# Dense blocks of 34 tiles from five node regions, in a two-layer graph network on one core

## The chip, the core and the metric

One core of a Trainium2 chip runs the whole program. The metric is the device time of one execution in microseconds (us); lower is better. TensorE multiplies matrices, VectorE and ScalarE work element by element, GpSimd (POOL) issues the gathers, SyncE (SP) issues most other DMAs.

## The reference

There are 12,500 nodes with 128 features and 200,000 edges with 64 attributes; `dst` is sorted, and dst = 12500 u^2 with u uniform, so nodes of low number have many edges and the rest few. Biases and weights of two layers follow.

```python
h = relu(layernorm(x))
for W_msg, Wih, Whh, bih, bhh in layers:                 # two
    msg = concat([h[src], edge_attr], -1) @ W_msg.T
    agg = segment_sum(msg, dst, 12500)
    h = gru_cell(agg, h, Wih, Whh, bih, bhh)
out = x + h
```

The kernel sums `h[src]` and `edge_attr` per node first and multiplies by `W_msg` afterwards, which is the same by linearity. `src` is random over all nodes.

## The kernel before, in words

**Edges.** A tile is 128 consecutive edges, a group four tiles (512 edges); there are 390 full groups and a last one of 320 edges. For a group VectorE makes one-hot matrices of each edge's node within a window of 80 columns (`onehot_of`, L1033 and L1036), TensorE multiplies attributes (L720, layer 0 only: the sum of attributes per node, `edgeT`, serves both layers) and gathered rows (L736) with them into PSUM, and VectorE adds the window into `edgeT` (L1098) and `aggT` (L1101).

**Gathers.** The rows `h[src]` of a group come by four indirect DMAs of 128 rows each, which GpSimd issues (L601) into a ring of six groups (`rows`). It waits for the group six gathers back to be summed and for the group's indices.

**Dense tiles.** The first 78 groups (312 tiles, nodes 0 to 494) are not gathered. All nodes' h lies in SBUF (`hr`, 100 tiles of 125 nodes), and one iteration of the main loop (13 per layer) treats a block of 24 dense tiles. For each tile a matrix A counts how many edges lead from each of the 12,500 nodes to each of 5 columns (nodes) of the tile: `lo_hot` (position within 125 nodes) times `v_hot` (which of the 100 node tiles, times column), made on VectorE (L1015, L1022) and multiplied on TensorE in packs of six tiles (`build_pack`, L689, bf16). ScalarE copies a pack from PSUM to `a_blk` (L1273). Then 100 multiplications of `a_blk` (120 columns) with `hr` (L696) accumulate the block's 120 rows in `ps_v`. This is done in eight slices of 12 or 13 node tiles. At the end ScalarE copies the rows (L1286), TensorE moves them into a window of 128 columns (L766) and VectorE adds it to `aggT` (L1125).

**Order of one iteration.** It is written out by `order(layer)`: 24 gathered groups (`gi` 0 to 23), in layer 0 with 6 attribute-only groups of dense edges between them. After gathered group gi, `divmod(gi, 3)` gives slice and phase: in phases 0 and 1 TensorE builds two packs each, in phase 2 it multiplies the slice. After every sixth gathered group (a step) the chunks whose nodes are complete are computed.

**Chunks.** A chunk is 250 nodes (50 in all): TensorE turns h (L811), multiplies messages (L815, L816) and six gate matrices (L819 to L828), ScalarE copies and applies sigmoid and tanh (L1333 to L1346), VectorE combines (L1178 to L1189), and TensorE turns the result back (`turn_back`, L800) when the next chunk starts. The result goes to a table in DRAM, from which layer 1 gathers, or to the output. `ready_i`, a table made on the chip, says after which step each chunk is ready. Chunks run in the order of nodes, rotated by `ROT`, so that those with dense nodes come last; `last_chunks` treats what is left behind the last group.

**Queues.** SP loads attributes, `dst_in` and indices into slots that come free when `group_summed` passes (`slot_free`), in the order of the groups. VectorE makes the one-hots of a group two places ahead of its addition (`onehot_after`).

**Start.** Layer norm of all nodes, storing them to `h_table` (the gathers wait for that), then tables of the groups' bases and of the dense tiles, made on VectorE from `dst` and `src` (L896 to L974). A tile wider than its columns, or a group wider than its window, would be done again in overflow passes, and all chunks would wait for them.

## Time and profile before

| | us |
|---|---|
| median of 3 runs | 3468.92 |
| lowest, highest | 3451.53, 3472.8 |
| profiled execution | 3465.33 |
| its span, first to last instruction | 3463.4 |
| busy: TensorE, VectorE, ScalarE, GpSimd | 2764.6, 1477.5, 1010.2, 2472.9 |

The profile is of one execution. Its rows name a line of the kernel, an engine, an operation and tiles; PE is TensorE's matmul, PEld its weight load, DVE VectorE, ACT ScalarE, POOL GpSimd. "Idle before" is the idle time of an engine ahead of such an instruction, with what released it; "issue" is time in which it waited for nothing that the profile shows. PEclk is the granted TensorE clock as a share of 2.4 GHz. An f32 matmul stands as two records, a bf16 one as one.

### The profile page before, as it was taken

Reading aid. Unit: us, or ns where it says so; the run is one execution under the profiler, and the core shown is the slowest. Engines: PE = TensorE matmul, PEld = TensorE weight load, DVE = VectorE, ACT = ScalarE, POOL = GpSimd, SP = SyncE. Lnnn points to the kernel's source line nnn. Section 1 sums busy time; section 2 is a strip of 40 time slices with the busy share of each in tenths; the row PEclk is TensorE's granted clock in tenths of the full one; section 3 lists DMA queues with packets and bytes.
Section 4 is the critical chain, followed back from the end, with each engine's and each line's share of the span. In section 5 each row is a group of like instructions: output and inputs, shape, how many; then the busy total and the mean of one; then the engine's idle time right before and its main releaser. Section 6 shows DMA issues by size and latency. Waiting matters only on the chain.

```text
span 3463.4 us, 74591 instructions
## 1 busy us (share of the span) xinstructions
PE 2764.6 (80%) x20436; PEld 2489.4 (72%) x20437; DVE 1477.5 (43%) x4429; ACT 1010.2 (29%) x2007; POOL 2472.9 (71%) x2544
## 2 busy tenths in 40 slices
PE   0788888988898998989867777778776878777886
PEld 0787877877887787778746767777776767766775
DVE  6543444444444444444423333333343444444443
ACT  5322222322233333332322122222222323233333
POOL 4677777777777777767527777777777777777772
PEclk9988888988988988988867677777787888888887
DMA  7333333333333333323233222222222222222221
GB/s 190 78 86 85 90 86 86 93 87 85 92 87 88 92 90 80 93 78 86 74 72 80 53 58 56 59 58 59 59 61 59 61 62 61 61 64 65 63 59 35
DMA packets 367262, 262.22 MB, mean 76 GB/s; under 512 B 239960, under 2 KB 325596, under 8 KB 366962
## 3 DMA queue, kind: packets, MB, share of 16 engines
q0 software_dynamic: 81376, 167.62, 17.8%
q1 hardware_dynamic: 264807, 70.52, 10.0%
q10 hardware_dynamic: 20779, 20.48, 2.0%
q8 instruction: 139, 2.28, 0.3%
q14 instruction: 161, 1.32, 0.1%
HBM read 239.14 MB, written 19.20 MB: 75 GB/s over the span
## 4 chain that ended last, share of the span: by engine, by line
PE 37%; POOL 31%; issue 16%; DVE 5%; ACT 3%; DMA 3%; DVEq 2%; ACTq 2%; POOLq 1%; SPq 0%
POOL rows L601 31%; PE ps_v L696 11%; PE ps_win L736 9%; PE ps_win L720 4%; PE ps_c L689 2%; PE ps_a L819 2%; PE ps_q L689 2%; DVEq L1093 1%; PE ps_c L823 1%; PE ps_c L821 1%; PE ps_b L824 1%; PE ps_d L826 1%; DMA rows<-h_table,idx 1%; ACT hr L1255 1%; PE ps_d L828 1%
## 5 line engine op out<-in xcount | busy, mean ns | idle before, releaser
L601 POOL DMA_INDIRECT rows<-h_table,idx x1252 | 1229.1, 982 | 481.9 <-issue 404.8
L601 POOL DMA_INDIRECT rows<-x_table,idx x1252 | 1219.0, 974 | 445.1 <-issue 433.9
L736 PE MATMUL ps_win<-onehot,rows 128*128 128x80 f32 x5008 | 801.8, 311 | 235.6 <-DMA rows<-x_table,idx 169.9
L736 PEld LDWEIGHTS ps_win<-onehot,rows 128*128 128x128 f32 x5008 | 716.8, 220 | 282.7 <-issue 169.2
L696 PE MATMUL ps_v<-hr,a_blk 125*120 125x128 f32 x5200 | 817.9, 330 | 0.0
L696 PEld LDWEIGHTS ps_v<-hr,a_blk 125*120 125x120 f32 x5200 | 796.8, 238 | 0.0
L1273 ACT COPY a_blk<-ps_q 125x390 f32<-125x390 f32 (+1 forms) x416 | 220.6, 530 | 1176.1 <-PE ps_q L689 1079.5
L1022 DVE SCALAR_TENSOR_TENSOR v_hot<-v_cur,lane 128x390 bf16<-128x390 f32 (+1 forms) x834 | 422.6, 544 | 0.0
L1101 DVE TENSOR_TENSOR aggT<-aggT,ps_win 128x80 f32 x626 | 143.8, 230 | 579.1 <-PE ps_win L736 520.8
L720 PE MATMUL ps_win<-onehot,attr 128*64 128x80 f32 x3128 | 317.7, 252 | 67.1 <-issue 44.0
L1036 DVE TENSOR_TENSOR onehot<-lane,rel 128x320 f32<-128x320 f32 x706 | 348.8, 494 | 24.2
L689 PE MATMUL ps_q<-v_hot,lo_hot 128*125 128x65 bf16 (+1 forms) x2496 | 226.6, 230 | 145.8 <-DVE v_hot L1022 141.0
L720 PEld LDWEIGHTS ps_win<-onehot,attr 128*64 128x64 f32 x3128 | 259.5, 148 | 102.8 <-issue 59.1
L1098 DVE TENSOR_TENSOR edgeT<-edgeT,ps_win 64x80 f32 x391 | 89.5, 229 | 560.0 <-PE ps_win L736 493.6
L689 PEld LDWEIGHTS ps_q<-v_hot,lo_hot 128*125 128x125 bf16 x2496 | 202.0, 151 | 161.8 <-DVE v_hot L1022 155.9
L1178 DVE SCALAR_TENSOR_TENSOR r_sb<-ps_a,bT,r_sb 128x250 f32<-128x250 f32 x100 | 47.8, 478 | 519.1 <-ACT r_sb L1337 300.7
L689 PE MATMUL ps_c<-v_hot,lo_hot 128*125 128x65 bf16 (+1 forms) x2496 | 236.8, 235 | 6.7 <-DVE v_hot L1022 6.7
L1273 ACT COPY a_blk<-ps_c 125x390 f32<-125x390 f32 (+1 forms) x416 | 220.5, 530 | 14.2 <-PE ps_c L689 10.5
L1273 ACT ACT_TABLE_LOAD x104 | 133.4, 1283 | 278.5 <-PE ps_q L689 277.4
L689 PEld LDWEIGHTS ps_c<-v_hot,lo_hot 128*125 128x125 bf16 x2496 | 199.5, 153 | 12.2 <-DVE v_hot L1022 8.5
L1033 DVE TENSOR_SCALAR rel<-dst_in,base_all 128x4 f32<-128x4 int32 x706 | 171.5, 243 | 12.1 <-issue 8.9
L1323 ACT ACT_TABLE_LOAD x100 | 128.3, 1283 | 89.3 <-issue 89.0
(178 smaller groups left out, 1940.8 us busy)
## 6 DMA issues: line engine op xcount, KB each, us to landing
attr<-in_edge_attr_dram SPq DMA_DIRECT2D x390, 128.0 KB
rows<-h_table,idx POOLq DMA_INDIRECT x1252
rows<-x_table,idx POOLq DMA_INDIRECT x1252
dst_in<-in_dst_dram SPq DMA_DIRECT2D x702, 2.0 KB
idx<-in_src_dram SPq DMA_DIRECT2D x624, 2.0 KB
x_table<-out_sb ACTq DMA_DIRECT2D x50, 125.0 KB
attr<-in_x_dram ACTq DMA_DIRECT2D x50, 125.0 KB
out_dram<-out_sb ACTq DMA_DIRECT2D x50, 125.0 KB
```

Source lines behind the costliest of these rows:

```text
L601: nc.gpsimd.indirect_dma_start(out=rows[0:parts, s, j, :], out_offset=None, in_=table[:, :], in_offset=bass.IndirectOffsetOnAxis(ap=idx[0: ...
L689: mm = nc.tensor.matmul((ps_q, ps_c)[k % 2][0:QUART, j * wide:(j + 1) * wide], lo_hot[:, k * PACK + j, :], v_hot[:, k % 2, j, 0:wide], sta ...
L696: mm = nc.tensor.matmul(ps_v[0:VC, 0:H], a_blk[:, t - slice_at[sl], :], hr[:, t, :], start=(t == 0), stop=(t == NT - 1))
L720: mm = nc.tensor.matmul(ps_win[r % 2][0:D, WIN:2 * WIN], attr[0:parts, r, j, :], onehot[0:parts, r % 2, j, :], start=(j == 0), stop=(j == ...
L736: mm = nc.tensor.matmul(ps_win[r % 2][:, 0:WIN], rows[0:parts, rr, j, :], onehot[0:parts, r % 2, j, :], start=(j == 0), stop=(j == TILES - 1))
L1022: return nc.vector.scalar_tensor_tensor(out=v_hot[:, k % 2, :, 0:wide], in0=cur[:, k * PACK:(k + 1) * PACK].unsqueeze(2).to_broadcast([P, ...
L1033: nc.vector.tensor_scalar(rel[:, s % 2, :], dst_in[:, s, :], float(N), base_all[:, bass.ds(g, 1)], ALU.min, ALU.subtract).then_inc(rel_rea ...
L1036: nc.vector.tensor_tensor(onehot[:, s % 2, :, :], lane[:, 0:WIN].unsqueeze(1).to_broadcast([P, TILES, WIN]), rel[:, s % 2, :].unsqueeze(2) ...
L1098: ins = nc.vector.tensor_tensor(e, e, ps_win[s % 2][0:D, WIN:2 * WIN], ALU.add)
L1101: ins = nc.vector.tensor_tensor(a, a, ps_win[s % 2][:, 0:WIN], ALU.add)
L1273: return nc.scalar.copy(a_blk[:, 0:n, k * PACK * W:(k + 1) * PACK * W].rearrange("p h (j w) -> p j h w", w=W), (ps_q, ps_c)[k % 2][0:QUART ...
L1323: nc.scalar.activation(scratch[:, :], zero[:, :], ACT.Sigmoid)
```

## The change

Dense tiles become 408 (102 groups, nodes 0 to 849), taken from five regions of nodes: a block has 8 tiles of 2 columns, 7 of 3, 8 of 4, 7 of 5 and 4 of 6, that is 34 tiles and 128 columns; its tiles of a region are consecutive, those of different regions far apart. There are 12 iterations for 13, and seven slices (14 or 15 node tiles) for eight, in the first 21 of 24 gathered places. A pack is a list of parts of regions (`PACK_TILES`), so each of VectorE's and ScalarE's operations on a pack becomes one per part: seven per slice for four. The block's window (now five pieces of `aggT`) moves from the end of the iteration to the 22nd gathered place. Of the 102 dense groups' attributes, 8 stand in each iteration and 6 (`HEAD`) ahead of the loop. The rings of attributes and `dst_in` shrink from six to four slots. ROT goes from 2 to 4. The tables at the start are made per region. In a chunk, the message matmuls come before the previous chunk's `turn_back`, `h_rows` is copied one chunk ahead, the result is written to `z_sb` rather than over `m_sb`, and a chunk starts when the previous one's `t_ready` has come. SP issues the last group's index load before its wait.

```diff
-ITERS = 13
+ITERS = 12
 SUBS = 4
 SLOTS = SUBS * RING
-ROT = 2
-W = 5
-BT = RING * TILES
-VC = BT * W
-PACK = 6
-PACKS = BT // PACK
-SLICES = 8
+ROT = 4
+AR = 4
+REGIONS = ((8, 2, 14), (7, 3, 20), (8, 4, 32), (7, 5, 36), (4, 6, 26))
+PACK_TILES = (((0, 0, 8), (1, 0, 6)), ((3, 6, 7), (4, 0, 4)), ((2, 0, 8),), ((1, 6, 7), (3, 0, 6)))
+NR = len(REGIONS)
+TILE_AT = [sum(n for n, w, c in REGIONS[:r]) for r in range(NR + 1)]
+ROW_AT = [sum(n * w for n, w, c in REGIONS[:r]) for r in range(NR + 1)]
+COL_AT = [sum(c for n, w, c in REGIONS[:r]) for r in range(NR + 1)]
+BT = TILE_AT[NR]
+VC = ROW_AT[NR]
+PACKS = len(PACK_TILES)
+SLICES = 7
+USED = 3 * SLICES
...
-    DENSE = ITERS * RING
+    DENSE = ITERS * BT // TILES
+    ATTR = SLOTS // (AR - 1)
+    HEAD = DENSE - ITERS * ATTR
...
-        dst_in = sb("dst_in", [P, RING, TILES], I32)
+        dst_in = sb("dst_in", [P, AR, TILES], I32)
         rel = sb("rel", [P, 2, TILES])
         rows = sb("rows", [P, RING, TILES, H])
-        attr = sb("attr", [P, RING, TILES, D])
+        attr = sb("attr", [P, AR, TILES, D])
...
-        v_hot = sb("v_hot", [P, 2, PACK, HS * W], BF16)
+        v_hot = sb("v_hot", [P, 2, HS * max(sum((b - a) * REGIONS[r][1] for r, a, b in rs) for rs in PACK_TILES)], BF16)
...
-            return [(q, None, q // 5) if q % 5 == 4 else (q, q - q // 5, None) for q in range(SLOTS + RING)]
+            return [(q, None, q // AR) if q % AR == AR - 1 else (q, q - q // AR, None) for q in range(SLOTS + ATTR)]
 
         def place(layer, it, q):
 
-            return it * len(order(layer)) + q
+            return it * len(order(layer)) + q + (0 if layer else HEAD)
...
+        def pack_parts(sl, k):
+
+            at = 0
+            for r, a, b in PACK_TILES[k]:
+                n, w = b - a, REGIONS[r][1]
+                wide = (slice_at[sl + 1] - slice_at[sl]) * w
+                yield TILE_AT[r] + a, ROW_AT[r] + a * w, n, w, wide, slice(at, at + n * wide)
+                at += n * wide
...
-                sp.wait_ge(group_summed, p + (layer * ORDERED[0] - RING + 1 + AHEAD))
+                sp.wait_ge(group_summed, p + (layer * ORDERED[0] - AR + 1 + AHEAD))
...
+                for t, row, n, w, wide, at in pack_parts(sl, k):
+                    for j in range(n):
+                        own = slice(at.start + j * wide, at.start + (j + 1) * wide)
+                        mm = nc.tensor.matmul((ps_q, ps_c)[k % 2][0:QUART, own], lo_hot[:, t + j, :],
+                                              v_hot[:, k % 2, own], start=True, stop=True)
                 return mm
...
-                    pe.wait_ge(h_ready, cc)
+                    pe.wait_ge(h_ready, cc + 1)
                     pe.wait_ge(chunk_done, cc)
                     for q in range(NQ):
-                        tr = nc.tensor.transpose(ps_t[:, q * P:(q + 1) * P], halves(m_sb[:, :])[:, q, :], ident[:, :])
+                        tr = nc.tensor.transpose(ps_t[:, q * P:(q + 1) * P], halves(z_sb[:, :])[:, q, :], ident[:, :])
                     tr.then_inc(h_turned, 1)
 
                 def chunk(i, groups_done, blocks_done, packs_done):
                     cc = layer * CHUNKS + i
                     c = chunk_at(i)
-                    with pe.If(i > 0):
-
-                        turn_back(cc)
-                    pe.wait_ge(h_rows_kept, cc + 1)
+                    pe.wait_ge(t_ready, cc + 1)
+                    pe.wait_ge(h_rows_kept, cc + (layer + 1))
...
+                    with pe.If(i > 0):
+
+                        turn_back(cc)
...
+                    for p in range(HEAD):
+                        attr_group(p, p % AR, p // AR)
...
+                            if gi >= USED:
+                                if gi == USED:
+                                    window_of_block(blk)
+                            elif phase < 2:
...
+            for r, (n, w, c) in enumerate(REGIONS):
+                for to, ps in ((lo_t, ps_a), (drel_t, ps_c)):
+                    nc.vector.tensor_copy(in_blocks(to[:, 0:NTILE])[:, :, tiles_of(r)], region_tiles(ps, r))
+                nc.vector.tensor_copy(in_blocks(hi_t[:, 0:NTILE])[:, :, tiles_of(r)], region_tiles(ps_b, r))
+                nc.vector.tensor_copy(in_blocks(tile_base)[:, :, tiles_of(r)], region_tiles(ps_d[0:1, :], r))
+                nc.vector.tensor_reduce(v_wide[:, :, r], region_tiles(ps_v[0:VC, :], r), AX.X, ALU.max)
+                nc.vector.tensor_reduce(v_min[:, :, r], region_tiles(ps_d[0:VC, :], r), AX.X, ALU.min)
+                nc.vector.tensor_reduce(v_max[:, :, r], region_tiles(ps_d[0:VC, :], r), AX.X, ALU.max)
+                nc.vector.tensor_reduce(region_of[:, r:r + 1], row_of[:, tiles_of(r)], AX.X, ALU.add)
+                ins = nc.vector.tensor_tensor(v_work[:, :, tiles_of(r)], region_tiles(ps_d[0:VC, :], r),
+                                              row_col[:, tiles_of(r)].unsqueeze(1).to_broadcast([VC, ITERS, n]), ALU.add)
...
+                for t, row, n, w, wide, at in pack_parts(sl, k):
+                    ins = nc.vector.scalar_tensor_tensor(
+                        out=v_hot[:, k % 2, at].rearrange("p (t c) -> p t c", c=wide),
+                        in0=cur[:, t:t + n].unsqueeze(2).to_broadcast([P, n, wide]),
+                        scalar=float(slice_at[sl] * w),
+                        in1=lane[:, 0:wide].unsqueeze(1).to_broadcast([P, n, wide]),
+                        op0=ALU.subtract, op1=ALU.is_equal)
...
+                    starts = [dve.value_load(window_base[0:1, bass.ds(it * NR + r, 1)], min_val=0, max_val=N) for r in range(NR)]
+                    added_before(p)
                     dve.wait_ge(v_summed, blk + 1)
-                    a = aggT[:, bass.ds(at, XWIN)]
-                    nc.vector.tensor_tensor(a, a, ps_v[:, 256:256 + XWIN], ALU.add).then_inc(acc_free, 1)
+                    for r, (n, w, c) in enumerate(REGIONS):
+                        a = aggT[:, bass.ds(starts[r], c)]
+                        if r:
+                            dve.drain()
...
-                    nc.vector.tensor_tensor(m_sb[:, :], m_sb[:, :], r_sb[:, :], ALU.add).then_inc(h_ready, 1)
-
-                for q in range(2):
...
+                    act.wait_ge(h_ready, cc + 1)
+                    act.wait_ge(hch_turned, cc + 1)
+                    nc.scalar.copy(h_ch[:, :], ps_h).then_inc(hch_kept, 1)
+                    act.wait_ge(msg_ready, cc + 1)
+                    nc.scalar.copy(m_sb[:, :], ps_m).then_inc(m_kept, 1)
...
+                    keep_rows(i + 1)
+                    if layer == 0:
+
+                        nc.scalar.copy(cols(aggT, c), zero[:, 0:1].to_broadcast([P, CHUNK])).then_inc(agg_cleared, 1)
```

## Rows read from the trace of the kernel before

**Rows 1.** The page, busy us, share of the span and instructions by engine.
```profile
PE 2764.6 (80%) x20436; PEld 2489.4 (72%) x20437; DVE 1477.5 (43%) x4429; ACT 1010.2 (29%) x2007; POOL 2472.9 (71%) x2544
```

**Rows 2.** Windows: length; PE, PEld, DVE, ACT, POOL busy (x); PEclk, DMA share, GB/s.
```profile
200.00:1200.00 1000.00, 875.88 (x7106) 794.00 (x7105) 447.78 (x1381) 272.78 (x538) 763.35 (x777) 0.86 0.34 88
1200.00:1743.00 543.00, 492.51 (x3797) 428.91 (x3795) 246.41 (x752) 177.83 (x362) 374.38 (x384) 0.87 0.32 82
1800.00:3200.00 1400.00, 1057.67 (x7318) 978.34 (x7318) 555.85 (x1509) 372.84 (x707) 1065.65 (x1095) 0.78 0.26 63
...
1655.00:1675.00 20.00, 19.24 (x201) 18.20 (x202) 12.15 (x39) 8.03 (x15) 13.46 (x14) 1.00 0.38 92
```

**Rows 3.** The page, costliest groups: busy, mean ns of one, idle before by releaser.
```profile
L601 POOL DMA_INDIRECT rows<-h_table,idx x1252 | 1229.1, 982 | 481.9 <-issue 404.8
...
L1022 DVE SCALAR_TENSOR_TENSOR v_hot<-v_cur,lane 128x390 bf16<-128x390 f32 (+1 forms) x834 | 422.6, 544 | 0.0
...
L1036 DVE TENSOR_TENSOR onehot<-lane,rel 128x320 f32<-128x320 f32 x706 | 348.8, 494 | 24.2
```

**Rows 4.** Timeline of TensorE: one step of layer 0 (start, length, line).
```profile
1654.89 0.77 PE L720 MATMUL ps_win<-onehot,attr 128*64 128x80 f32 x8
...
1667.64 0.48 PE L689 MATMUL ps_q<-v_hot,lo_hot 128*125 128x60 bf16 x6
...
1668.40 0.77 PE L720 MATMUL ps_win<-onehot,attr 128*64 128x80 f32 x8
...
1675.14 0.47 PE L800 MATMUL ps_d<-ident,m_sb 128*125 128x128 f32 x2
```

**Rows 5.** Timeline of TensorE: the matmul that ends a block, two layers.
```profile
214.38 0.49 PE L766 MATMUL ps_v<-v_onehot,v_rows 120*128 120x128 f32 x2
...
1455.56 0.49 PE L766 MATMUL ps_v<-v_onehot,v_rows 120*128 120x128 f32 x2
...
1742.91 0.49 PE L766 MATMUL ps_v<-v_onehot,v_rows 120*128 120x128 f32 x2
...
3154.17 0.49 PE L766 MATMUL ps_v<-v_onehot,v_rows 120*128 120x128 f32 x2 [0.36 <-ACT v_rows L1286]
...
3410.15 0.49 PE L766 MATMUL ps_v<-v_onehot,v_rows 120*128 120x128 f32 x2 [0.36 <-ACT v_rows L1286]
```

**Rows 6.** Who GpSimd waited for in layer 0: us, times, longest.
```profile
POOL rows L601 <- PE ps_win L736: 60.3, 71, 9.3
```

**Rows 7.** Timeline of VectorE in the table stage, and of GpSimd at the first wait.
```profile
83.18 0.17 DVE L946 COPY lo_t<-ps_a 128x24 f32<-128x24 f32 x1
...
84.81 0.48 DVE L949 TENSOR_REDUCE aggT<-ps_v 120x13 f32<-120x312 f32 x1
...
110.88 1.14 POOL L601 DMA_INDIRECT rows<-h_table,idx  x1 [8.50 <-PE ps_win L736]
```

**Rows 8.** Timeline of TensorE: two chunks in one step of layer 0.
```profile
1640.58 0.47 PE L800 MATMUL ps_d<-ident,m_sb 128*125 128x128 f32 x2
...
1648.30 0.50 PE L800 MATMUL ps_d<-ident,m_sb 128*125 128x128 f32 x2 [2.71 <-DVE m_sb L1189]
```

**Rows 9.** Weight loads by line: count, ns min/median/max, first and last start, shapes.
```profile
L696 PEld LDWEIGHTS ps_v<-hr,a_blk x5200: 183/183/324, 119.4 to 3409.4; 125*120 125x120 f32 x193
...
L736 PEld LDWEIGHTS ps_win<-onehot,rows x5008: 186/192/338, 108.1 to 3422.6; 128*128 128x128 f32 x192, 80*128 80x128 f32 x1
```

**Rows 10.** Chunks at a layer's end: two starts in layer 0, one loop in layer 1.
```profile
1770.01 0.79 PE L800 MATMUL ps_d<-ident,m_sb 128*125 128x128 f32 x2 [2.68 <-DVE m_sb L1189]
...
1780.40 0.79 PE L800 MATMUL ps_d<-ident,m_sb 128*125 128x128 f32 x2 [2.68 <-DVE m_sb L1189]
...
3441.75 0.37 ACT L1333 COPY h_ch<-ps_a 128x250 f32<-128x250 f32 x1 [2.28 <-issue]
...
3448.76 0.42 DVE L1189 TENSOR_TENSOR m_sb<-m_sb,r_sb 128x250 f32<-128x250 f32 x1
```

**Rows 11.** The chain that ended last, around the first gather of layer 1.
```profile
1791.96 2.58 DMA x_table<-out_sb
```

312 lines of the change are left out of this document (181 added, 131 removed).

## Prediction

> **What bounds the kernel now.** I read the busy shares first, and they name the wrong engine: TensorE 80% of the span, GpSimd 71% [rows 1]. Stretches by stage correct this. From 200 to 1200 us GpSimd issued 777 gathers, one every 1.287 us; from 1800 to 3200 us 1095, one every 1.279 us [rows 2]. The costliest groups show why: an indirect DMA keeps GpSimd 0.98 us, and 404.8 us of issue (0.3 us for most) stand before 1252 of them, with no releaser named [rows 3]. So GpSimd never rests there, although its share is only 0.76: the 0.3 us is not counted as busy. TensorE has slack: where its granted clock is 1.00 [rows 2], one step (six gathered groups, two slices of the block) takes it 20.3 us, from 1654.89 to 1675.14 [rows 4], so an iteration of four steps 81 us without chunks, while its 96 gathers take 123 us.
>
> Late in layer 0 this turns. The matmul of L766, which ends each block, stands at 214.38, 1455.56 and 1742.91 us [rows 5]: the last two iterations take 143.7 us each, and the twelve together 1528.5 us where 12 x 96 x 1.279 is 1473. The excess is 55 us. GpSimd's own waits agree: 60.3 us for TensorE in this layer [rows 6], of which 8.5 stand at the start [rows 7]. Nodes per edge grow with the edge number, so the chunks (the GRU of 250 nodes) crowd at the end. Two in one step cost TensorE 14.3 us (1640.58 to 1654.89 [rows 8, 4]), 2.7 of them waiting for the first one's result. In layer 1 the marks 3154.17 and 3410.15 enclose two iterations of 128.0 us [rows 5], together 10 us over their gathers.
>
> **1. Gathers removed: -246 us.** Dense tiles go from 312 to 408, so gathered groups from 24 x 13 to 24 x 12 in each layer: 24 groups of 4 DMAs fewer. 96 x 1.287 + 96 x 1.279 = 246.3 us [rows 2], all on the path as long as GpSimd sets the pace. A gather's rows are as long as before, so its price stays.
>
> Does everything fit? I counted on the inputs that the reference draws: no tile is wider than its region's 2, 3, 4, 5 or 6 nodes, in no block does a region reach over its 14, 20, 32, 36 or 26 columns (the most are 9, 14, 23, 27 and 18), and no group spans 80 nodes. So no overflow pass runs, before or after. The chunks per step, counted in the same way, keep their pattern (2, 1, 2, 1 in the last iteration); five instead of three are left for the end, as ROT goes from 2 to 4.
>
> **2. Start: +17 us (8 to 26).** The gathers begin at the same time: they wait for the stored h_table. But 24 DMAs fill the ring, and GpSimd then waits 8.50 us for the first group to be summed [rows 7]. That group comes later now, and nothing hides it, since the ring is full. First the tables: about 45 VectorE operations by region replace ten over 312 columns; one over 24 columns takes 0.17 and one over 312 takes 0.48 us [rows 7], so 84 or 96 columns about 0.22, and 45 x 0.22 - 10 x 0.48 is +5; some 15 more small ones add 3. I take +8 (bounds 3 and 12, if they overlap more or less than those rows). Then six groups of edge attributes stand ahead of the first gathered one. On TensorE one takes 0.77 us at full clock [rows 4] and under twice that at half; on VectorE the one-hot of the group two places on takes 0.49 [rows 3] and its two neighbours about as much together. Six at 1.5 us are 9 (bounds 5 and 14).
>
> **3. TensorE's work per iteration: +5 us, hidden except late.** Packs: 34 x 7 = 238 small matmuls for 192, in 28 packs for 32. A pair of packs takes 0.76 us (1667.64 to 1668.40, 12 matmuls) [rows 4]; split as 0.053 a matmul and 0.12 a pair that is 14.3 for 12.2, +2.1 (1 if all is per pack, 3 if all is per matmul). Two more attribute groups of 0.7: +1.4. The hundred multiplications load 128 weight columns for 120: the medians of such loads are 192 and 183 ns [rows 9], 200 records, +1.5 to +1.8. VectorE: 49 v_hot operations for 32, on 12,800 columns for 12,000: 32 x 0.544 = 17.4 [rows 3] grows to between 18.6 and 21.5 us (17 more starts of 0 to 0.17), and lo_hot of ten more tiles brings it to about +5 in an iteration of 123 us of which VectorE works 45%. That and ScalarE's copies in two parts lie beside gathers; late in layer 0, where they would not, I count nothing for them and leave the upper end of the range to them.
>
> **4. Chunks reordered: -3 and -4 us.** The message matmuls come ahead of turn_back, h_rows is copied one chunk ahead, and the result goes to z_sb, so a second chunk's front no longer waits for the first one's end. What is left as a loop runs from the copy of h_ch to the last VectorE operation, 3441.75 to 3449.18, 7.4 us; starts now are 10.4 us apart (1770.01, 1780.40) [rows 10]. So each double step of layer 0 (five of them, two in the last iteration) gains 3 us, and the window, moved to the 22nd gathered place, takes about 2 us of waiting off each iteration's end. Against them stand the +5 us of part 3, 6 with its stretches at half clock: the last iteration comes out at 143.7 + 6 - 2 - 6 = 142 us, and the 55 us of excess at about 52: -3. The same in layer 1, without attributes, makes 6 of 10: -4.
>
> **5. Ends of the layers: -2 us.** Five chunks of 7.4 for three of 10.4: +6 a layer. The last three gathered groups carry no pack or multiplication any more, and the last step's chunk need not wait for the block's sum: -4 in layer 0, where TensorE lags by a whole ring, -10 in layer 1, where it lags by one multiplication. The tail's index load ahead of SP's wait frees GpSimd earlier, which is worth nothing: TensorE is later.
>
> **6. Slower gathers: +6 us.** VectorE is busy 448 of 1000 us in layer 0 and 556 of 1400 (397 in 1000) in layer 1, and a gather takes 8 ns longer in layer 0 [rows 2]. Part 3 adds some 4.5 points of VectorE to both: at most 7 ns on 2312 gathers, 16 us; 0 if the 8 ns come from the attribute transfers, and below that if the ring of four spreads these better, which nothing here prices. I take 6.
>
> **Sum:** -246 + 17 - 3 - 4 - 2 + 6 = -232. The profiled execution took 3465.3 us (span 3463.4 and 1.9 around it); the median of the runs is 3468.9, 0.1% above it. 3465.3 - 232 = 3233 us.
>
> **Rivals.**
> - **TensorE takes over (14%).** The chunk reordering gains nothing while part 3 costs its 6 us per iteration. Then the last two iterations take 150 instead of 142 (+16), the three before them 135 instead of 126 (+27), and layer 1 keeps its 10 us (+4): 3233 + 47 = 3280. For it: TensorE is 0.91 busy from 1200 us on [rows 2]. Against it: 2.7 us of each double step are plain waiting [rows 8].
> - **Its stalls vanish (8%).** Late in layer 0 the granted clock is 0.87 [rows 2]. If TensorE pauses so little that it stays at 2.4 GHz, four steps of 21.5 us and six chunks of 5 to 7 fit into the gathers' 123 us, and 45 of the 52 us go: 3188.
> - **Ports (6%).** Each added microsecond of VectorE stops GpSimd for as long: 5 x 24 = 120 us, 0.78 of it beside gathers, 94 less the 6 already counted: 3321. Against it: 51 us more of VectorE in 1000 would then lengthen a gather by 65 ns, and the difference of the layers is 8 [rows 2].
> - **Slower: the ring of four (4%).** SP may load dst_in only two places ahead of VectorE's need, not four. Places pass in 3.84 us in layer 0 (123 / 32) and 5.1 in layer 1. From a free slot to the landed data 2 x 3.84 less 1 us for VectorE are hidden, 6.7 us; beyond, half of the excess is paid on each of 391 places. From 7.9 us the 232 us are used up: 3465, and 3500 at 8.1. Against it: the nearest row is a store of 125 KB that landed 2.6 us after its issue [rows 11].
> - **It does not fit (1%).** One tile over its width would send every chunk behind the last gather: 2 x 45 x 7.4 = +666. The count on the inputs excludes it.
>
> On "ports" the Trainium skill has a rule that speaks against this change. SBUF — State Buffer, "Who interferes with whom", says that a VectorE instruction with two SBUF inputs, or in a two-port mode, and a GpSimd instruction that needs the shared ports exclude each other for a whole instruction; the added one-hots have two SBUF inputs. By that rule the sum would be the rival's, 3321; this case's 8 ns bear out little of it, by which it is 3233.
>
> [...]
>
> **Chances and range.** My forecast has 67% and a range of its own, 3205 to 3260 (start 8 to 26, chunk period 6 to 9, excess 40 to 65 us). The whole range goes from "stalls vanish" with the cheaper start, 3180, to "TensorE takes over" with the dearer start and 16 us of slower gathers, 3310 rounded; ports, ring and misfit, 11%, stay outside. Faster by over 1%: 0.95; within 1%: 0.02; slower by over 1%: 0.03. About 1% is what a measurement of this kernel tells from no change.
>
> **What would show it.** Right: 1156 gathers per layer, one each 1.28 to 1.295 us; GpSimd's wait at the start 24 to 27 us; block marks 123 us apart until the eighth iteration and 138 to 145 in the last two of layer 0; five chunks at each layer's end 7 to 8 us apart; layer 1's first gather at about 1691 us (1795.6 - 123.6 + 17 - 3 + 2 + 3). Wrong: waits of VectorE for dst_in, a mean gather over 1.0 us, marks more than 130 us apart in layer 1.

## The result, and the profile after

The changed kernel takes 3280.1 us in the median of four runs (3269.6 to 3287.8), the kernel before 3465.7 us (four runs): a ratio of 0.9467, 95% interval 0.9426 to 0.9508. That is 186 us less. The forecast was 3233 us, 232 less than before's profiled execution; the time lies in its range (3180 to 3310) and above the likeliest case's own range (3205 to 3260). In the profiled execution the time is 3279.4 us, its span 3277.7.

The page of the kernel after: busy time by engine (against [rows 1]), then its costliest groups (against [rows 3]: busy, mean ns of one, idle before).

```profile
PE 2630.1 (80%) x20375; PEld 2360.7 (72%) x20376; DVE 1530.0 (47%) x4895; ACT 999.1 (30%) x2343; POOL 2324.6 (71%) x2389
...
L666 POOL DMA_INDIRECT rows<-h_table,idx x1156 | 1153.2, 998 | 485.3 <-issue 376.2
L666 POOL DMA_INDIRECT rows<-x_table,idx x1156 | 1144.5, 990 | 410.4 <-issue 402.1
...
L1115 DVE SCALAR_TENSOR_TENSOR v_hot<-v_cur,lane 128x42 bf16<-128x42 f32 (+13 forms) x1180 | 435.1, 425 | 0.0
...
L1130 DVE TENSOR_TENSOR onehot<-lane,rel 128x320 f32<-128x320 f32 x682 | 338.2, 496 | 23.4
```

The gathers are 1156 for 1252 in each layer, but each keeps GpSimd 998 and 990 ns instead of 982 and 974. Windows of the kernel after, the columns as in [rows 2]:

```profile
200.00:1200.00 1000.00, 886.69 (x7442) 799.41 (x7442) 492.82 (x1597) 284.81 (x674) 761.56 (x765) 0.86 0.35 89
1200.00:1660.00 460.00, 412.64 (x3412) 361.74 (x3412) 230.13 (x735) 157.82 (x372) 315.89 (x319) 0.90 0.33 84
1800.00:3200.00 1400.00, 1103.20 (x7962) 1008.21 (x7961) 616.46 (x1823) 412.67 (x952) 1070.14 (x1083) 0.79 0.24 60
```

A gather starts every 1.307 us in layer 0's first stretch and every 1.293 in layer 1, for 1.287 and 1.279 before. VectorE is busy 4.5 points more, as forecast. The rest shows in GpSimd's start, its waits (us in total, times, longest) and the matmul that ends each block, now L832, whose start is called a block's mark below (against [rows 7], [rows 6] and [rows 5]):

```profile
82.71 0.94 POOL L666 DMA_INDIRECT rows<-h_table,idx  x1 [0.30 <-issue]
117.79 1.12 POOL L666 DMA_INDIRECT rows<-h_table,idx  x1 [34.14 <-PE ps_win L786]
```
```profile
POOL rows L666 <- PE ps_win L802: 49.7, 77, 7.7
POOL rows L666 <- PE ps_win L786: 36.0, 7, 34.1
POOL rows L666 <- DMA idx<-in_src_dram: 31.7, 6, 13.4
```
```profile
226.41 0.43 PE L832 MATMUL ps_v<-v_onehot,v_rows 128*128 128x128 f32 x2
...
1377.31 0.43 PE L832 MATMUL ps_v<-v_onehot,v_rows 128*128 128x128 f32 x2
...
1520.86 0.43 PE L832 MATMUL ps_v<-v_onehot,v_rows 128*128 128x128 f32 x2
...
1660.00 0.43 PE L832 MATMUL ps_v<-v_onehot,v_rows 128*128 128x128 f32 x2
...
3217.04 0.43 PE L832 MATMUL ps_v<-v_onehot,v_rows 128*128 128x128 f32 x2
```

GpSimd stops after 8 gathers (82.71 is the eighth), not after 24, for 34.14 us. The last two iterations of layer 0 take 143.6 and 139.1 us (forecast: 142), but the nine before them 127.9 each (1377.31 less 226.41, by nine), where 123 was forecast up to the eighth. The first and last gathers of each layer give the account:

```profile
L666 POOL DMA_INDIRECT rows<-h_table,idx x1156: 892/944/1869, 73.0 to 1665.8; - x193
L666 POOL DMA_INDIRECT rows<-x_table,idx x1156: 896/944/1877, 1723.1 to 3220.8; - x193
```

Before, these times were 72.5 to 1736.3 and 1795.6 to 3400.4, and the span ended at 3463.4.

| stretch, us | before | after | change | forecast |
|---|---|---|---|---|
| start to first gather | 72.5 | 73.0 | +0.5 | 0 |
| layer 0, first to last gather | 1663.8 | 1592.8 | -71.0 | -106.6 |
| to layer 1's first gather | 59.3 | 57.3 | -2.0 | with the end: -2 |
| layer 1, first to last gather | 1604.8 | 1497.7 | -107.1 | -123.7 |
| to the end | 63.0 | 56.9 | -6.1 | |

So layer 0 fell short by 36 us and layer 1 by 17, and the ends gave 6 more than forecast.

### The profile page after: what moved, and what is told of

Read it like the earlier page. It is cut to its first block, busy times and chain, and to the rows that moved or that the text cites. A ratio compares the mean times of both kernels' runs of the same rounds, so it can differ in the third digit from the quotient of the medians.

```text
span 3277.7 us, 74395 instructions
## 1 busy us (share of the span) xinstructions
PE 2630.1 (80%) x20375; PEld 2360.7 (72%) x20376; DVE 1530.0 (47%) x4895; ACT 999.1 (30%) x2343; POOL 2324.6 (71%) x2389
## 3 DMA queue, kind: packets, MB, share of 16 engines
q1 hardware_dynamic: 254617, 70.47, 10.3%
## 4 chain that ended last, share of the span: by engine, by line
PE 35%; POOL 30%; issue 16%; DVE 6%; DVEq 4%; DMA 3%; ACT 3%; ACTq 1%; SPq 1%; POOLq 1%
POOL rows L666 30%; PE ps_v L762 9%; PE ps_win L802 8%; PE ps_win L786 4%; PE ps_q L755 3%; DVEq L1187 2%; PE ps_c L755 2%; PE ps_b L879 1%; PE ps_b L880 1%; PE ps_d L866 1%; PE ps_d L895 1%; ACT hr L1366 1%; PE ps_a L886 1%; DVEq L1217 1%; PE ps_c L888 1%
## 5 line engine op out<-in xcount | busy, mean ns | idle before, releaser
L666 POOL DMA_INDIRECT rows<-h_table,idx x1156 | 1153.2, 998 | 485.3 <-issue 376.2
L666 POOL DMA_INDIRECT rows<-x_table,idx x1156 | 1144.5, 990 | 410.4 <-issue 402.1
L762 PE MATMUL ps_v<-hr,a_blk 125*128 125x128 f32 x4800 | 715.2, 319 | 0.0
L762 PEld LDWEIGHTS ps_v<-hr,a_blk 125*128 125x128 f32 x4800 | 698.4, 235 | 0.8
L1385 ACT COPY a_blk<-ps_q 125x224 f32<-125x224 f32 (+5 forms) x504 | 223.8, 480 | 856.3 <-PE ps_q L755 763.7
L1115 DVE SCALAR_TENSOR_TENSOR v_hot<-v_cur,lane 128x42 bf16<-128x42 f32 (+13 forms) x1180 | 435.1, 425 | 0.0
L755 PE MATMUL ps_q<-v_hot,lo_hot 128*125 128x28 bf16 (+5 forms) x3696 | 289.4, 222 | 139.9 <-DVE v_hot L1115 117.7
L755 PEld LDWEIGHTS ps_q<-v_hot,lo_hot 128*125 128x125 bf16 x3696 | 272.5, 151 | 151.2 <-DVE v_hot L1115 128.9
L1385 ACT COPY a_blk<-ps_c 125x70 f32<-125x70 f32 (+7 forms) x672 | 208.3, 376 | 15.1 <-PE ps_c L755 11.1
L755 PE MATMUL ps_c<-v_hot,lo_hot 128*125 128x70 bf16 (+3 forms) x2016 | 200.3, 244 | 6.5 <-DVE v_hot L1115 6.5
```

Source lines behind the costliest of these rows:

```text
L666: nc.gpsimd.indirect_dma_start(out=rows[0:parts, s, j, :], out_offset=None, in_=table[:, :], in_offset=bass.IndirectOffsetOnAxis(ap=idx[0: ...
L755: mm = nc.tensor.matmul((ps_q, ps_c)[k % 2][0:QUART, own], lo_hot[:, t + j, :], v_hot[:, k % 2, own], start=True, stop=True)
L762: mm = nc.tensor.matmul(ps_v[0:VC, 0:H], a_blk[:, t - slice_at[sl], :], hr[:, t, :], start=(t == 0), stop=(t == NT - 1))
L1115: ins = nc.vector.scalar_tensor_tensor(out=v_hot[:, k % 2, at].rearrange("p (t c) -> p t c", c=wide), in0=cur[:, t:t + n].unsqueeze(2).to_ ...
L1385: ins = nc.scalar.copy(a_blk[:, 0:hs, row:row + n * w].rearrange("p h (j w) -> p j h w", w=w), (ps_q, ps_c)[k % 2][0:QUART, at].rearrange( ...
```

## The experiments

Eleven edited kernels ran, and the changed kernel once more (e12_after_again), in three sets of four: e1 to e4, e5 to e8, e9 to e12. Each set has the kernel before timed on the same chip (3472.6, 3464.1 and 3467.7 us), so sets are compared by the ratio to it.

### A wait of the first iteration, and the indices

The place of a group in the order of sums counts the six head groups now. For gathered groups 2 to 5 of the first iteration this makes the wait for a free slot of rows a wait for sums of head groups, though the slots are empty. The first edit drops it; the second loads next iteration's indices earlier.

```diff
+                        if layer == 0 and gi < RING:
+                            with pool.If(it > 0):
+                                pool.wait_ge(group_summed, place(layer, it, rows_free(gi)) + (1 + AHEAD))
+                        else:
+                            pool.wait_ge(group_summed, place(layer, it, rows_free(gi)) + (layer * ORDERED[0] + 1 + AHEAD))
```


> The kernel after, with one edit: in layer 0's first iteration the first six gathered groups no longer wait for sums of the head attribute groups (their slots of rows are empty then). Theory (the unplanned part of the loss at the start is this wait): GpSimd issues 24 gathers instead of 8 before it first waits, that wait falls from 34.1 us to 20 to 25, the first block mark moves from 226.4 to about 218 us and the whole is 8 to 9 us shorter (about 3271 against 3279). Rival (TensorE, with the head groups ahead of its first gathered group, sets the pace there): the first block mark stays within 2 us of 226.4, later waits for TensorE take what the first gives, and the time stays within 3 us.

```diff
-                        if gi == SLOTS - 1:
+                        if gi == SLOTS - (1 if layer else 4):
```


> The kernel after, with one edit: in layer 0 the edge indices of the next iteration's first six groups are loaded after the loads for gathered group 20 and not after those for group 23, so that they wait for the sum of place 22 and not of place 26. Theory: the waits of GpSimd for indices inside the loop (18.3 us in five) are a loss of their own, since with a ring of four the index load of the next iteration is issued two sums later than its slot of rows comes free; they vanish and layer 0's gathers end 8 to 12 us earlier. Rival: TensorE is what is late there; the same time shows up as waits for ps_win, and the time stays within 3 us.

e1_start: 3276.4 us, ratio 0.943 (0.9409 to 0.9451); e2_idx: 3283.3 us, 0.9453 (0.9419 to 0.9488). Both intervals overlap the changed kernel's. In e1_start GpSimd issues its 24 gathers and then waits once:

```profile
102.29 0.94 POOL L666 DMA_INDIRECT rows<-h_table,idx  x1 [0.30 <-issue]
125.36 1.90 POOL L666 DMA_INDIRECT rows<-h_table,idx  x1 [22.12 <-PE ps_win L806]
```

The first block mark stands at 216.8 us for 226.4. Yet the ninth mark is at 1244.0 in e1_start and 1243.9 after, and layer 0's last gather ends at 1667.9 for 1666.7: the lead is given back in the eighth and ninth iteration. GpSimd's first wait is 12 us shorter, its later waits in layer 0 are 8 us longer together. The theory was right on the wait; of the time it named, this trace keeps nothing, though the ratio (0.943 for 0.9467) leaves up to 13 us open. In e2_idx the waits for indices vanish (31.7 us in total become 0.3). The tail's 13.1 us come back as a wait with no releaser named, those for TensorE grow from 49.7 to 58.4, and what is left, 8 us in layer 0, is met by gathers that are 7 us longer in sum in that profile; so little is within what two profiles of one kernel differ. The rival fits: in layer 0 something other than GpSimd is late.

### Is it TensorE's work?

This kernel leaves half of the edge attributes out of layer 0's sums, so it doesn't compute the reference; it is run for its time.

```diff
                 def attr_sums(r, parts):
-                    for j in range(TILES):
+                    for j in range(2):
```


> The kernel after, but TensorE sums the attributes of only two of the four tiles of each group in layer 0 (half of the edge attributes are left out of the sums); transfers, one-hots and additions stay. TensorE works some 10 us less in each of layer 0's iterations, nothing else changes. Theory (from about 900 us on TensorE sets layer 0's pace, which is why what GpSimd gained at the start was given back): the waits of GpSimd for ps_win in the loop nearly vanish, block marks are 126 us apart or less to the end, and layer 0's gathers, 1593.7 us in all after, take 1550 to 1560. Rival (GpSimd sets it, and the waits are noise of the ring): they take over 1580. Layer 1 stays as it is by both.

e5_light: 3289.3 us, ratio 0.9497 (0.948 to 0.9514), layer 0's gathers 1599.1 us to the end of the last (1593.7 in the changed kernel). Nothing is gained, as the rival has it, but its reason, waits that are noise, is not shown: GpSimd's waits in layer 0 after the first add up to 65.7 us for 54.4. Windows of e5_light:

```profile
200.00:1200.00 1000.00, 872.32 (x6423) 784.00 (x6424) 492.79 (x1594) 285.38 (x672) 758.93 (x763) 0.78 0.34 88
1200.00:1660.00 460.00, 406.35 (x2933) 356.14 (x2932) 228.78 (x727) 157.79 (x370) 313.09 (x319) 0.82 0.32 84
```

TensorE has 14% fewer matmuls in each stretch and is busy only 2% less, since the granted clock is 0.78 and 0.82 there for 0.86 and 0.90. A lower mean is more time at 1.2 GHz. So the run doesn't tell the two apart; the last two iterations take 140.4 and 141.0 us from mark to mark, together about as long as without the edit.

### The order of the chunk, both ways

The chunk's old order in the changed kernel, and the new order in the kernel before. The core of the edit, as e9_b_newchunk has it (e6_oldchunk has it backwards):

```diff
-                    with pe.If(i > 0):
-                        turn_back(cc)
...
                                      start=False, stop=True).then_inc(msg_ready, 1)
+                    with pe.If(i > 0):
+                        turn_back(cc)
...
+                    keep_rows(i + 1)
...
-                    nc.vector.tensor_tensor(m_sb[:, :], m_sb[:, :], r_sb[:, :], ALU.add).then_inc(h_ready, 1)
+                    nc.vector.tensor_tensor(z_sb[:, :], m_sb[:, :], r_sb[:, :], ALU.add).then_inc(h_ready, 1)
```


> The kernel after with the chunk in the order of before (turn_back first, h_rows copied in the chunk itself, the result in m_sb). Theory: the starts of chunks at the layers' ends are 10 us apart again for 5.7 to 6.3, which makes 20 us at each end; double steps of layer 0 take 3 to 6 us more, 15 to 25 us in layer 0; with 1 to 5 in layer 1 the whole is 55 to 70 us longer. Rival (the order gains only at the ends, since inside the loop something else is late): 35 to 45 us longer, layer 0's gathers within 5 us of 1593.7.

> The kernel before with the new order of the chunk and nothing else of the change (dense blocks of 24 tiles as before). Taking the order away from the changed kernel cost 130 us (74 in layer 0's gathers, 19 between the layers, 13 in layer 1's gathers, 28 at the end). Theory A (the order shortens the chain of waits in every chunk, in either kernel): block marks of the last two iterations of layer 0 fall from 143.5 to 131 to 136 us, layer 0's gathers by 35 to 60 us, chunk starts at the ends are 6 us apart, and the time is 70 to 105 us less than before, 3360 to 3395. Theory B (my prediction's terms: 3 us for each double step and each chunk at an end): 35 to 45 us less, about 3425. Theory C (the order only pays for what the new blocks cost TensorE): layer 0's gathers within 10 us of 1664.8, the whole 15 to 25 us less.

The columns are the order of the chunk, and "blocks of 34 tiles" stands for all the rest of the change:

| us, and ratio to before | old order | new order |
|---|---|---|
| blocks of 24 tiles | 3467.7 | 3400.9, 0.9807 (0.9793 to 0.9821) |
| blocks of 34 tiles | 3408.8, 0.9836 (0.9811 to 0.986) | 3275.8, 0.9456 (0.9437 to 0.9475) |

This is the main finding. By the ratios (e6_oldchunk is of another set) the new blocks alone are worth 57 us, the new order alone 67, both together 189. Without the order the blocks take away 246 us of gathers and keep less than a quarter of it. Both expectations (at most 70 us) were too small for e6_oldchunk, which takes 129 us longer than the changed kernel, and e9_b_newchunk fell between A and B, near A. The order has several parts (the message matmuls ahead of turn_back, `h_rows` copied ahead, the result in z_sb); none was run alone. Starts of the message matmul at a layer's end (layer 0), first before's order in e6_oldchunk, then the new one in the kernel after:

```profile
1770.24 1.04 PE L881 MATMUL ps_b<-aggT,wT 128*128 x2
...
1780.65 1.05 PE L881 MATMUL ps_b<-aggT,wT 128*128 x2
```
```profile
1699.76 0.68 PE L879 MATMUL ps_b<-aggT,wT 128*128 x2
...
1705.49 0.68 PE L879 MATMUL ps_b<-aggT,wT 128*128 x2
...
1711.13 0.68 PE L879 MATMUL ps_b<-aggT,wT 128*128 x2
```

10.4 us become 5.7, and the message matmul itself takes 0.68 for 1.05 us: over these chunks the granted clock is 1.00, where it is 0.68 in the old order. Windows of the kernel after, then of e6_oldchunk:

```profile
1695.00:1712.00 17.00, 14.82 (x61) 9.65 (x60) 6.51 (x16) 12.58 (x31) 0.00 (x0) 1.00 0.08 24
```
```profile
1765.00:1802.00 37.00, 26.27 (x72) 18.31 (x70) 8.62 (x20) 17.00 (x38) 0.00 (x0) 0.68 0.04 10
```

TensorE, busy 0.87 of the time for 0.71, stays at 2.4 GHz. In layer 0's six steps with two chunks, TensorE needs 18.3 us in the mean before and 12.1 in e9_b_newchunk (from the end of the instruction before the chunks to the start of the one behind). That is 37 us, and layer 0's gathers end 37.5 us earlier there. GpSimd's waits in that layer (from 120 us on):

```profile
POOL rows L601 <- PE ps_win L736: 51.5, 69, 9.3
POOL rows L601 <- DMA idx<-in_src_dram: 15.8, 3, 13.9
```
```profile
POOL rows L601 <- PE ps_win L736: 21.7, 55, 5.3
POOL rows L601 <- DMA idx<-in_src_dram: 0.3, 1, 0.3
```

The first pair is the kernel before, the second e9_b_newchunk: GpSimd sets the pace nearly to the end, with the last two iterations at 129.3 and 128.4 us. Against that, the changed kernel's 143.6 and 139.1 show what the new blocks add late in layer 0: 11 to 14 us an iteration (10 and 11 in a second profile), where the prediction's part 3 had 5 to 6. The ring of four and ROT are in this difference too; neither was run alone.

### Where the new blocks cost TensorE

In layer 0 (226 to 1650 us) TensorE waits 62.0 us for one-hots in the changed kernel and 9.3 in e9_b_newchunk (us, times, longest):

```profile
PE ps_win L786 <- DVE onehot L1130: 62.0, 46, 5.1
```
```profile
PE ps_win L720 <- DVE onehot L1039: 9.3, 9, 1.1
```

VectorE and TensorE around the 22nd gathered place of the tenth iteration:

```profile
1380.14 0.49 DVE L1130 TENSOR_TENSOR onehot<-lane,rel 128x320 f32<-128x320 f32 x1
1383.92 0.17 DVE L1224 TENSOR_TENSOR aggT<-aggT,ps_v 128x14 f32 x1 [3.29 <-issue]
1384.26 0.18 DVE L1224 TENSOR_TENSOR aggT<-aggT,ps_v 128x20 f32 x1 [0.16 <-issue]
...
1385.28 0.18 DVE L1224 TENSOR_TENSOR aggT<-aggT,ps_v 128x26 f32 x1 [0.15 <-issue]
1386.52 0.23 DVE L1192 TENSOR_TENSOR edgeT<-edgeT,ps_win 64x80 f32 x1 [1.06 <-issue]
```
```profile
1381.39 1.12 PE L802 MATMUL ps_win<-onehot,rows 128*128 128x80 f32 x8
1387.62 1.33 PE L786 MATMUL ps_win<-onehot,attr 128*64 128x80 f32 x8 [5.12 <-DVE onehot L1130]
```

add_block reads five starts from a table into registers and adds five pieces with a drain between them. VectorE shows no work for 3.29 us, needs 1.54 for the pieces and stands idle for 1.06 behind them. None of the 3.29 us is a wait: add_block waits for the block's matmul, which ended at 1377.7, and for VectorE's own last addition, which ended at 1379.9, both before the 3.29 us begin. The same 3.27 to 3.31 us stand ahead of the first piece in all 24 blocks of both profiles of the changed kernel and of e10_winend below. In the kernel before, where there is one start to read, 0.42 or 0.43 us stand there in each of layer 0's 13 blocks:

```profile
339.23 0.29 DVE L1125 TENSOR_TENSOR aggT<-aggT,ps_v 128x128 f32 x1 [0.43 <-issue]
```

The four more reads are all that the code has more ahead of the first addition, so about 0.7 us each is an estimate ((3.29 - 0.43) / 4); no run changes the reads alone. The next one-hot is late by all this, and TensorE waits 5.12 us. Moving the block's end:

```diff
-                        if gi == USED:
-                            add_block(it, blk, place(layer, it, q + 1))
...
                         last = q + 1 == len(order(layer))
+                        if last:
+                            add_block(it, blk, place(layer, it, q + 1))
```


> The kernel after with the block's last matmul and the five additions moved from the 22nd gathered place back to the iteration's end. Theory (the prediction's): chunks of the last step and the next block wait for them, 2 us in each of layer 0's late iterations and nothing where GpSimd sets the pace: 4 to 12 us longer. Rival: the additions in the middle hold back one-hots as much as they do at the end: within 4 us.

e10_winend: 3285.9 us, ratio 0.9478 (0.9464 to 0.9491), beside 3275.8 and 0.9456 for the changed kernel in the same set. The intervals overlap, the medians are 10 us apart: the theory's 4 to 12 us fit, but no gain or loss is shown. The stall is only moved. In e10_winend TensorE waits 50.5 us for aggT (9 times, up to 5.8), while its waits for one-hots fall to 28.1. Reading the five starts earlier, before anything waits for them, was not tried.

### What lengthens a gather

> The kernel after, with VectorE drained after each piece of lo_hot and v_hot: the same operations and columns, but no two of them back to back. Theory 1 (an unbroken run of VectorE operations with two inputs in SBUF holds GpSimd's gather until it ends, so the loss grows faster than the run's length): the mean gather falls from 994 ns to 975 or less, those above 1200 ns from 174 to under 90, and the time falls by 20 to 40 us less what TensorE takes back in layer 0. Theory 2 (the busy time or the number of VectorE's operations counts): the mean gather stays within 4 ns of 994. Theory 3 (DMA or TensorE traffic lengthens them): the same as theory 2.

> The kernel after, with each piece of lo_hot and v_hot made by two operations of half the tiles, back to back: the same columns, twice the operations, runs a few per cent longer. Theory 1 (unbroken runs count): the mean gather stays within 5 ns of 994, or rises with the runs' length. Theory 2 (the number of operations counts): it rises by 10 ns or more, 23 us in all. A fourth theory, that one long operation (lo_hot of eight tiles, 1.20 us) is what holds a gather, and a gap of itself lies between two operations: it falls to 980 or less.

e3_gaps adds this, behind each piece of lo_hot, between the pieces of v_hot and behind the last; e4_split makes each piece by two calls over half the tiles, as e8_losplit below.

```diff
+                    dve.drain()
```

e3_gaps: 3361.6 us, 0.9687 (0.9667 to 0.9708). e4_split: 3296.4 us, 0.9494 (0.9475 to 0.9513). The mean gather stays at 993.3 ns in the first, with 154 gathers above 1200 ns for 174 (under 90 by theory 1), and rises to 996.8 in the second. Theory 1, of unbroken runs, falls: the gaps are there and change nothing, while the drains make the kernel slower, layer 0's gathers by 46 us and layer 1's by 12. In e4_split neither theory 2's rise of 10 ns nor the fourth's fall to 980 came. The rows show what holds a gather. VectorE and GpSimd of the kernel after, at its longest gather:

```profile
2489.25 1.20 DVE L1108 TENSOR_TENSOR lo_hot<-lane,lo_t 128x1000 bf16<-128x1000 f32 x1
2490.36 0.62 DVE L1115 SCALAR_TENSOR_TENSOR v_hot<-v_cur,lane 128x448 bf16<-128x448 f32 x1
```
```profile
2489.38 1.88 POOL L666 DMA_INDIRECT rows<-x_table,idx  x1 [0.30 <-issue]
```

The gather starts at 2489.38, while the lo_hot of 1.20 us runs. It ends at 2491.26, which is 0.81 us after the end of that operation (2490.45), and the v_hot that follows back to back doesn't hold it. Of the gathers that take at least 30 ns more than 944 (the median), 535 of 538 in this trace and 575 of 579 in before's end 0.80 to 0.84 us after the end of a VectorE operation, nearly always one with two inputs in SBUF, and in every one of these that operation was under way when the gather started. So a gather waits for the operation that it meets at its start. What an operation costs should then grow about with the square of its length: the chance to be met, times the mean rest. As an estimate from these rows, with starts spread evenly and only a rest over 0.12 us counted (0.94 us is the median, 0.82 the time behind the operation), lo_hot would hold gathers for 26 us before, 38 after, 55 in e7_lojoin and 20 in e8_losplit. The table below has 13, 28 to 35, 36 and 14: the order is about right and the sizes are not, so the square is no price. The limit of this shows in e4_split, where operations begin only 0.2 us apart: 22 gathers there are held past the one they met, the longest, 2.92 us, over nine, and these make 24.7 of its 122.0 us over 944 ns. Short pieces in a close row pay back what they save.

Two more kernels change that length for lo_hot alone:

```diff
-                for r, a, b in PACK_TILES[k]:
-                    n, t = b - a, TILE_AT[r] + a
+                for t, n in (((0, 14),), ((29, 5),), ((15, 8),), ((14, 1), (23, 6)))[k]:
```
(e7_lojoin), and in e8_losplit

```diff
-                for r, a, b in PACK_TILES[k]:
+                for r, a, b in [p for r, a, b in PACK_TILES[k]
+                                for p in ((r, a, (a + b) // 2), (r, (a + b) // 2, b)) if p[2] > p[1]]:
```


> The kernel after, with the pieces of lo_hot that are neighbours made by one operation (14 tiles in one, 5 in one): the same columns in fewer operations, the longest about 2.1 us for 1.2. In the traces so far nearly every long gather ends 0.82 us after the end of a VectorE operation with two inputs in SBUF that was under way at the gather's start, even where another follows back to back. Theory 1b (a gather waits for the one operation under way, so what an operation costs grows with the square of its length): gathers held by lo_hot lose about 40 us for 27.9, the mean gather rises from 994 to 998 or more and some take over 2.5 us. Theory 1 (unbroken runs) and theory 2 (busy time): the mean stays within 2 ns.

> The kernel after, with each piece of lo_hot made by two operations of half the tiles and v_hot left whole. Theory 1b: gathers held by lo_hot lose 14 to 18 us for 27.9, the mean gather falls from 994 to 988 to 991, layer 1's gathers end 3 to 6 us earlier. Theory 1 (unbroken runs): no change, or more with the 40 added operations' starts. Rival (gathers freed from lo_hot are caught by the next operation of v_hot): lo_hot's share falls, v_hot's rises by as much, and the mean stays within 2 ns of 994.

Summed over all gathers, the time over 944 ns and what held them, in us:

| kernel | over 944 ns | by onehot | by v_hot | by lo_hot (count, mean ns) | mean gather, ns |
|---|---|---|---|---|---|
| before | 84.3 | 29.5 | 34.6 | 13.4 (106, 933) | 978 |
| after | 115.1 | 42.8 | 36.0 | 27.9 (172, 786) | 994 |
| after, again | 117.5 | 41.5 | 33.8 | 35.0 (172, 784) | 995 |
| e7_lojoin | 115.7 | 39.1 | 32.0 | 36.1 (122, 1044) | 994 |
| e8_losplit | 104.9 | 42.5 | 40.9 | 13.5 (295, 521) | 989 |

e8_losplit bears the theory out in the rows: 3270.6 us, 0.9431 (0.9407 to 0.9455), lo_hot's share halves and layer 1's gathers take 5.5 us less; v_hot takes 5 to 7 us of it, 9 gathers being held from a piece of lo_hot on into v_hot. Its ratio alone is not apart from the changed kernel's: the intervals overlap. e7_lojoin doesn't decide: 3283.4 us, 0.9475 (0.9457 to 0.9492), its 36.1 is no more than the unchanged kernel showed in a second profile. Its longest gather shows the mechanism once more (727.73 + 2.48 is 0.83 after 727.41 + 1.97):

```profile
727.41 1.97 DVE L1107 TENSOR_TENSOR lo_hot<-lane,lo_t 128x1750 bf16<-128x1750 f32 x1
```
```profile
727.73 2.48 POOL L666 DMA_INDIRECT rows<-h_table,idx  x1 [0.30 <-issue]
```

Why fewer one-hots of the same length (496 ns for 494) hold gathers for 42.8 us where it was 29.5 stays open; the mean delay rises from 131 to 169 ns, which points to where in a gather they fall.

### A version that beats both

The edits of e1_start, e2_idx and e8_losplit, and the tail's indices, loaded inside the last iteration:

```diff
+                            with sp.If(it > ITERS - 2):
+                                sp.dma_start(idx[0:REST, 0, 0, :], edges(src, FULL, REST)).then_inc(idx_loaded[0][0], 16)
...
-                sp.dma_start(idx[0:REST, 0, 0, :], edges(src, FULL, REST)).then_inc(idx_loaded[0][0], 16)
```


> The kernel after with four edits together: no wait for the head groups in the first iteration, indices of the next iteration loaded earlier in layer 0, those of the last partial group loaded inside the last iteration, lo_hot in pieces of half the tiles. By the single runs the pieces give 9 us; the start and the indices gave nothing in one profile each, since layer 0's late iterations took back what they gained; the last one takes away a wait of 13 us whose gather TensorE may not need that early. Theory: 3262 to 3272 us, 8 to 18 less than the kernel after in the same call. Rival (the gains add up once the pieces also shorten VectorE's part): 3245 to 3258.

> The changed kernel itself once more, beside the three others on the same chip: within 0.3% of 3280 us, mean gather 994 ns within 2, layer 1's gathers 1497 to 1500 us. It is the yardstick for e10_winend and e11_best, and shows how far two profiles of one kernel differ.

e11_best takes 3256.2 us, ratio 0.9392 (0.9379 to 0.9405), the changed kernel beside it 3275.8 us and 0.9456 (0.9437 to 0.9475): the intervals are apart, and the medians by 19.5 us; the two profiles differ by 10.3. That is a little more than the theory had (8 to 18 us less) and inside the rival's 3245 to 3258, in which the gains add up. Gathers of e11_best:

```profile
L667 POOL DMA_INDIRECT rows<-h_table,idx x1156: 897/945/1747, 72.8 to 1639.7; - x193
L667 POOL DMA_INDIRECT rows<-x_table,idx x1156: 903/945/1746, 1709.9 to 3200.7; - x193
```

Layer 0's last gather starts 18.5 us earlier than in the second profile of the changed kernel (1658.2), layer 1's first only 6.4 (1716.3): the tail's early index mostly moves a wait. The last block mark of layer 0 stands at 1647.0 us for 1654.9 in e8_losplit alone, so some of the lead from the start seems to be kept here; that is hardly more than two profiles differ. Layer 1 from first to last is 1490.8 for 1497.5 us, the shorter lo_hot. Two profiles of the changed kernel differ by 6.5 us (3277.7 and 3271.2), 7.1 less in layer 0's gathers, so no profile alone shows a gain below that.

## Why the prediction was right, and where it was not

The bound, the sign and the main term hold: 192 gathers fewer, at 0.98 us and 0.305 of issue each, are 246 us (part 1). The profiled time missed by 46 us, and the case that was given 67% missed its own range (3205 to 3260). That the whole range held is owed to its width: its upper side was drawn for the rival "TensorE takes over", which did not occur. (That side also adds up to 3299, 3280 + 9 + 10, not to 3310; the time is inside both.) The terms, one by one:

- **Start (part 2): right for TensorE, wrong for GpSimd.** VectorE's first one-hot is at 115.0 us for 106.3 (+8.7; forecast 8), the six head groups last from 115.7 to 124.2 us (8.5; forecast 9), and TensorE's first gathered matmul moves from 108.1 to 124.2: 16 for the forecast 17. GpSimd loses 25.6 instead (34.14 less the 8.50 of [rows 7]), since I took the ring to fill ahead as before and did not put the new place numbers into the wait for rows. In e1_start's trace these 9 us are given back later, so they may not be what the forecast lacked.
- **TensorE's part of the blocks (part 3): too small.** I counted instructions on TensorE and nothing for VectorE. The marks late in layer 0 say 10 to 14 us an iteration for 5 to 6. Some 5 of it (62.0 us in twelve iterations) are waits for one-hots, the longest behind add_block's five starts and five additions, which the diff shows and my part 3 left out. The rest of it is not taken apart.
- **The new order (part 4): the mechanism right, the size half.** 3 us a double step was the change of the chunk's period, from 10.4 to 7.4; measured are 6.2. The step that I read, 14.3 us, was the shortest; layer 0 has six, not the five that I counted, and they take 18.3 in the mean. My 55 us of excess took layer 1's 1.279 us a gather; with layer 0's own 1.287 it is 46, which is what GpSimd's waits there add up to behind the first (45.9). In the last two iterations this error and part 3's nearly cancel: 142 us were forecast for the last iterations, 143.6 and 139.1 came. The iterations before them did not cancel: 130.6, 133.1, 127.2 and 133.4 from the seventh to the tenth, where I had 123 to 126. GpSimd's waits in layer 0 behind the first rose by 9 us (45.9 to 54.4) where 3 less were forecast: 12 us of the miss. In the second profile of the changed kernel they are 45.0, so 9 of these 12 are no more than two profiles differ.
- **Ends (part 5): better.** Five chunks 5.7 us apart at full clock, not 7.4: -8 for -2.
- **Slower gathers (part 6): the term most mis-sized.** 16 ns on 2312 gathers are 37 us, 6 were forecast with 16 as the upper end: 31 of the 46 us. I scaled 8 ns, a difference of two layers, by VectorE's busy time; what counts is the operation that a gather meets at its start, and how long it still runs. By the table, lo_hot's pieces, the longest 1.20 us for 0.93, hold gathers 15 to 22 us more than before; the one-hots 12 to 13 more, at the same length, and why is open. The "ports" rival had the mechanism and the wrong price. The Trainium skill's page SBUF — State Buffer, "Who interferes with whom", says that a VectorE instruction with two SBUF inputs contends with a GpSimd instruction that reads SBUF (a gather reads `idx` there), and calls the shared ports an exclusive lock. The rows above agree, with one addition: a gather is held by what it meets at its start, so VectorE's 45 us more in 1000 cost 16 ns a gather and not the 58 that this rival's one for one would make of them.
- **The rival "TensorE takes over"** gave 3280, which is the time measured, by another road: it had the reordering gain nothing, and e6_oldchunk puts that case at 3409. Its marks (150 us in the last two iterations) did not come.
- **The ring of four** never makes VectorE wait: no wait for dst_in is in the trace. Its price came elsewhere, as waits for idx, which are loaded behind it; e2_idx shows them to cost nothing that two profiles could tell. "It does not fit" did not happen.
- **The signs.** Held: 1156 gathers per layer, and 143.6 and 139.1 us in the last two iterations (138 to 145). Missed: GpSimd's wait at the start, 34.1 us for 24 to 27; a gather each 1.307 us in layer 0 for 1.295 at most; 128 us between marks where 123 were forecast; chunks at the ends 5.7 us apart for 7 to 8; layer 1's first gather at 1723.1 us for 1691. None of the signs of being wrong came.

The account: 31 (gathers) + 9 (start) + 12 (late waits) - 6 (ends) = 46. That these add up says where in the trace the time lies, not what each is worth: in e1_start's trace the 9 are lost in layer 0 anyway. In the second profile, 40 us over the forecast, the same terms are 34, 9, 2 and -5, so gathers and start hold in both profiles and the late waits do not.

What stays open: which engine sets the pace from the seventh iteration on. The signs point to the chain through a chunk and the block's end, over TensorE, VectorE and ScalarE, by e6_oldchunk, e9_b_newchunk and the waits; that TensorE's amount of work sets it was not shown, as e5_light was met by a lower clock. Of the 74 us that the old order costs layer 0 in the new kernel, the double steps explain 23 (17.2 for 13.4 us, six times); the rest is not placed.

## What to carry to other kernels

Where two parts of a change touch the same late stretch, price each with the other absent, then both together: here 57 and 67 us alone make 189 together. Count an engine's register reads and the drains between dependent additions as work: they show as "issue", not as busy, and hold up the next operand. Beside indirect gathers, split the long two-input VectorE operations (1.2 us here), not all of them: the rows show fewer held gathers, though the time alone was not apart from noise. Put new place numbers into every wait that uses them, empty ring included.

## Of the hardware, not expected

- An indirect gather that starts during a VectorE operation with two SBUF inputs ends 0.80 to 0.84 us after that operation (535 of the 538 long gathers of this trace): 2.48 us for the usual 0.94 behind one of 1.97 us. Where pieces start 0.2 us apart it can miss the gaps and wait over nine (2.92 us).
- With 14% fewer matmuls on TensorE the granted clock fell from 0.86 to 0.78, and the time stayed (e5_light).
- Where VectorE reads five starts from a table into registers ahead of an addition, 3.27 to 3.31 us pass without work in every block, with all waits met; with one read it is 0.42 or 0.43 us (kernel before, layer 0).
